# Moving GpSimd's work within a round of a product-key experts kernel, with wider pick sums and a later split of W_down

## The reference, cut to what matters

```python
q = (x @ Wq + bq).reshape(B, S, 8, 64)            # x = layernorm(x1)
s1 = einsum(q[..., :32], K1); s2 = einsum(q[..., 32:], K2)      # 64 scores each
v1, i1 = top_k(s1, 10); v2, i2 = top_k(s2, 10)
all_scores = v1[..., :, None] + v2[..., None, :]   # 100 sums a head
vals, best = top_k(all_scores, 10)                 # expert = i1 * 64 + i2
scores = softmax(vals)
h = gelu(x . W_down[expert]) * scores              # 8 heads x 10 experts
out = sum(h * W_up[expert])
result = x1 + layernorm(out)
```

## Time and profile before

| | us |
|---|---|
| median of 3 runs | 3631.82 |
| lowest, highest | 3631.26, 3637.74 |
| profiled execution | 3642.26 |
| its span | 3640.5 |

### The profile page before, as it was taken

How to read it: one execution, slowest core, us unless ns; L and a number is a source line. 1 busy time by engine, 2 the same in 40 slices (tenths; PEclk the granted TensorE clock), 3 DMA queues, 4 the chain that set the end, 5 groups by cost and what they waited for, 6 DMA issues and landing times. The chain is left out here.

```text
span 3640.5 us, 92336 instructions
## 1 busy us (share of the span) xinstructions
PE 3229.7 (89%) x31732; PEld 2786.5 (77%) x31732; DVE 3126.5 (86%) x15084; ACT 2134.9 (59%) x4411; POOL 2137.0 (59%) x1790
## 2 busy tenths in 40 slices
PE   5999999951499999999999899999999999999988
PEld 3666666631388888888888888888888888888888
DVE  5566666544899999999999999999999999999972
ACT  3444444411576766666666676666666666776662
POOL 1333333333366767666666677767766666676674
PEclk9999999975589999989988899989999888898988
DMA  2111111123033333333333333333333333333332
GB/s 62 47 53 53 53 53 53 41 76 156 30 117 116 118 118 114 103 104 116 103 103 119 104 126 115 120 114 109 103 117 103 103 103 120 120 119 111 117 117 97
DMA packets 132334, 356.93 MB, mean 98 GB/s; under 512 B 13865, under 2 KB 61609, under 8 KB 129452
## 3 DMA queue, kind: packets, MB, share of 16 engines
q1 hardware_dynamic: 131868, 351.03, 28.9%
HBM read 309.01 MB, written 25.17 MB: 92 GB/s over the span
## 5 line engine op out<-in xcount | busy, mean ns | idle before, releaser
L1182 PE MATMUL b_ps_a<-b_wup,b_hid 128*128 128x256 f32 x4096 | 955.9, 379 | 0.0
L1171 PE MATMUL b_ps_h<-b_xT_hi,b_wd_split 128*128 128x256 f32 x4096 | 931.8, 312 | 24.8 <-ACT b_hid L1322 21.5
L1010 POOL TENSOR_TENSOR b_hid<-b_hid,b_gates 128x512 f32<-128x512 f32 x512 | 717.4, 1401 | 297.1 <-ACT b_hid L1322 291.1
L1182 PEld LDWEIGHTS b_ps_a<-b_wup,b_hid 128*128 128x128 f32 x4096 | 743.4, 190 | 84.4 <-POOL b_hid L1010 0.3
L1171 PEld LDWEIGHTS b_ps_h<-b_xT_hi,b_wd_split 128*128 128x128 f32 x4096 | 709.2, 202 | 40.4 <-issue 31.1
L1301 ACT ACTIVATE b_ohq<-b_q_no,b_minus_qid 80x128 f16<-80x128 f16 x2048 | 648.1, 390 | 1.0
L1026 POOL TENSOR_TENSOR b_ohq<-b_qT 80x512 f16<-80x512 f16 x512 | 615.5, 1203 | 7.7 <-DVE b_qT L1422 7.7
L1171 PE MATMUL b_ps_h<-b_xT_lo,b_wd_split 128*128 128x256 f32 x2048 | 601.4, 294 | 0.0
L1098 PE MATMUL b_ps_s<-b_ohr,b_ohq 80*128 80x32 f16 x16384 | 445.4, 183 | 151.5 <-issue 151.3
L1098 PEld LDWEIGHTS b_ps_s<-b_ohr,b_ohq 80*128 80x128 f16 x16384 | 437.0, 101 | 158.3 <-issue 157.5
L1217 ACT ACTIVATE b_gates<-b_ps_s 128x512 f32<-128x512 f32 x512 | 305.6, 597 | 295.3 <-PE b_ps_s L1098 288.5
(11 more groups left out here) (192 smaller groups left out, 5518.0 us busy)
## 6 DMA issues: line engine op xcount, KB each, us to landing
b_wd_split<-wd_parts SPq DMA_DIRECT2D x512, 512.0 KB, 3.5
a_keysh<-a_key SPq DMA_DIRECT2D x16, 896.0 KB, 5.4
a_x<-in_x SPq DMA_DIRECT2D x16, 512.0 KB, 4.9
x_between<-a_y SPq DMA_DIRECT2D x16, 512.0 KB, 3.2
b_x<-x_between SPq DMA_DIRECT2D x32, 256.0 KB, 2.7
wd_parts<-b_wd_split SPq DMA_DIRECT2D x16, 512.0 KB, 3.1
b_x1t<-x_between SPq DMA_DIRECT2D x32, 256.0 KB, 4.1
out<-b_y SPq DMA_DIRECT2D x32, 256.0 KB, 2.3
```

Source lines behind the costliest of these rows:

```text
L1010: G.tensor_tensor(hid[:, p % 4, :, :], hid[:, p % 4, :, :], gates[:, 2 * p:2 * p + 2, :], ALU.mult).then_inc(mix_done, 1)
L1171: mm = T.matmul(hbank[p % 2][:, j * C:(j + 1) * C], a, c, start=i == 0, stop=i == len(parts) - 1)
L1182: mm = T.matmul(abank[:, t * D:(t + 1) * D], hid[:, p % 4, j, t * P:(t + 1) * P], wup[:, 2 * p + j, :], start=p == 0 and j == 0 and t == 0 ...
```

## The change

Six things are done together.

- GpSimd does 13 of the 16 mixes. VectorE does `mix(m, 13)` after the mask, `mix(m, 14)` after the product and `mix(m, 15)` after `onehots_r(m+1, 0)`. GpSimd's one-hot rows go in 13 portions of 5 tokens (the last of 4).
- On GpSimd `add_input(m-1)`, `low_x(m+2)` and `norm_in(m+3)` go behind mixes 0, 1 and 2; the first two thereby come a round later. SyncE's store and residual load move to p = 7 and 8.
- `sum_picks` takes three planes in one matmul: 9 matmuls of 480 columns. ScalarE copies three times as many columns, and `turn_picks` has 6 matmuls in place of 2, with 16-bit weights at a stride of six values.
- ScalarE's `soften(m+2)` goes ahead of `keep_gates(m+1)`; VectorE's goes from the lists of the next round to the end of the round; `turn_gates` goes from p = 4 to p = 1.
- The split of W_down: pieces 0 to 7 in round -2, pieces 8 to 15 in round -1, on ScalarE, GpSimd and SyncE. W_up is loaded after it.
- `low_gates` comes after pair 5 in place of 6, ahead of the one-hot portion.

```diff
-AT_GATES = 4
-AT_GLO, AT_CID = 6, 10
+AT_GATES = 1
+POOL_MIXES, DVE_MIXES = 13, 3
+WIDE = 3
+AT_GLO, AT_CID = 5, 10
...
         load(0)
-        keep_parts()
+        load_wdown()
         for m in range(-3, chunks + 1):
...
+            if m in (-3, -2):
+                keep_parts(m + 3)
+            if m == -2:
+                parts_kept()
...
-        for p in range(PAIRS_R):
-            low_down(p)
         for m in range(-3, chunks + 1):
             if has(m + 3):
                 root(0, m + 3)
-            if has(m + 3):
-                norm_in(m + 3)
-            for p in range(PAIRS_R):
+
+            if m in (-2, -1):
+                for p in range((m + 2) * PAIRS_R // 2, (m + 3) * PAIRS_R // 2):
+                    low_down(p)
+            for p in range(POOL_MIXES):
                 if has(m):
                     mix(m, p)
-                if has(m + 1):
-                    onehots(m + 1, p)
+                if p == 0 and has(m - 1):
+                    add_input(m - 1)
+                if p == 1 and has(m + 2):
+                    low_x(m + 2)
+                if p == 2 and has(m + 3):
+                    norm_in(m + 3)
                 if p == AT_GLO and has(m + 1):
                     low_gates(m + 1)
                 if p == AT_CID and has(m + 2):
                     pair_numbers(m + 2)
-            if has(m + 3):
-                low_x(m + 3)
+                if has(m + 1):
+                    onehots(m + 1, p)
             if has(m):
                 root(1, m)
-                add_input(m)
...
-            for c in range(NPAIR):
-                mm = T.matmul(rows, ident16[:, :], pk[:, :, c, :], start=c == 0, stop=c == NPAIR - 1)
+            for c in range(0, NPAIR, WIDE):
+                mm = T.matmul(rows, ident16[:, :], pk[:, :, c:c + WIDE, :], start=c == 0, stop=c == NPAIR - WIDE)
...
             for t in range(NT):
-                mm = T.matmul(mbank[0][0:SLOTS, t * P:(t + 1) * P], picked[:, t, :], ident16[:, :], start=True, stop=True)
+                for c in range(WIDE):
+                    mm = T.matmul(mbank[0][0:SLOTS, t * P:(t + 1) * P], picked[:, :, c, t], ident16[:, :],
+                                  start=c == 0, stop=c == WIDE - 1)
...
             if has(m + 3):
                 scores(m + 3)
+            if has(m + 2):
+                soften(m + 2)
             if has(m + 1):
                 for b in range(BLOCKS):
                     keep_gates(m + 1, b)
-            if has(m + 2):
-                soften(m + 2)
...
+        def mix(m, p):
+            dve.wait_ge(gelu_done, m * PAIRS_R + p + 1)
+            dve.wait_ge(gates_done, GROUPS * (m + 1))
+            V.tensor_tensor(hid[:, p % 4, :, :], hid[:, p % 4, :, :], gates[:, 2 * p:2 * p + 2, :], ALU.mult).then_inc(mix_dve_done, 1)
...
-            if has(m + 1):
-                soften(m + 1)
...
-                pick(m + 2)
+                mask(m + 2)
+            if has(m):
+                mix(m, POOL_MIXES)
+            if has(m + 2):
+                product(m + 2)
+            if has(m):
+                mix(m, POOL_MIXES + 1)
             if has(m + 1):
                 onehots_r(m + 1, 0)
+            if has(m):
+                mix(m, POOL_MIXES + 2)
+            if has(m + 1):
                 onehots_r(m + 1, 1)
                 onehots_q(m + 1, 2)
...
             if has(m + 1):
                 onehots_r(m + 1, 3)
+            if has(m + 2):
+                soften(m + 2)
```

More of the change, by code:

```diff
@@ L831, in experts_phase @@
     posf = sb("b_posf", [P, SLOTS, NT], F16)
-    picked = sb("b_picked", [P, NT, SLOTS], F16)
+    picked = sb("b_picked", [P, SLOTS, WIDE, NT], F16)
     gate = sb("b_gate", [P, NT, SLOTS], F32)
@@ L877, in experts_phase @@
     ohq_pool_done, cid_done, glo_done = (sem(f"b_{n}") for n in ("ohq_pool", "cid", "glo"))
+    mix_dve_done = sem("b_mix_dve")
     eps_done = [sem(f"b_eps{i}") for i in range(2)]
@@ L935, in load, with load_wdown, keep_parts, parts_kept @@
             sp.dma_start(x1[:, :, :], x1_view[m]).then_inc(x1_in, 16)
-        def keep_parts():
+        def load_wdown():
             sp.dma_start(wdown, w["wdown"].rearrange("(k p) r q -> p k r q", p=P)).then_inc(wdown_in, 16)
-            sp.dma_start(wup[:, :, :], w["wup"]).then_inc(wup_in, 16)
-            for p in range(PAIRS_R):
+        def keep_parts(half):
+            for p in range(half * PAIRS_R // 2, (half + 1) * PAIRS_R // 2):
                 sp.wait_ge(wd_lo_done, p + 1)
                 sp.dma_start(wd_dram[p], whole_slot(p)).then_inc(wd_out[p % WD_SLOTS], 16)
+        def parts_kept():
+            sp.dma_start(wup[:, :, :], w["wup"]).then_inc(wup_in, 16)
             for i in range(WD_SLOTS):
@@ L968, in sp_program @@
                     load_down(m, p)
-                if p == 1 and has(m - 1):
+                if p == 7 and has(m - 1):
                     store(m - 1)
-                if p == 2 and has(m):
+                if p == 8 and has(m):
                     load_residual(m)
@@ L1019, in onehots @@
         def onehots(m, p):
-            n = BLK // PAIRS_R
-            tok = slice(p * n, (p + 1) * n)
-            shape = [SLOTS, n, 16, 8]
+            tok = slice(p * 5, min(p * 5 + 5, BLK))
+            shape = [SLOTS, tok.stop - tok.start, 16, 8]
             pool.wait_ge(oh16_done, m + 1)
@@ L1086, in gate_matrix @@
             if b == 0:
-                pe.wait_ge(ohq_pool_done, PAIRS_R * (m + 1))
+                pe.wait_ge(ohq_pool_done, POOL_MIXES * (m + 1))
             elif b == 1:
@@ L1115, in sum_picks @@
             pk = work.rearrange("p (s c t) -> p s c t", s=SLOTS, c=NPAIR)
-            rows = mbank[1][:, 0:NT * SLOTS].rearrange("p (s t) -> p s t", t=NT)
+            rows = mbank[1][:, 0:NT * WIDE * SLOTS].rearrange("p (s c t) -> p s c t", c=WIDE, t=NT)
             pe.wait_ge(picks_done, m + 1)
@@ L1175, in up @@
             n = m * PAIRS_R + p
-            pe.wait_ge(mix_done, n + 1)
+            if p < POOL_MIXES:
+                pe.wait_ge(mix_done, POOL_MIXES * m + p + 1)
+            else:
+                pe.wait_ge(mix_dve_done, DVE_MIXES * m + p - POOL_MIXES + 1)
             pe.wait_ge(wup_in, 16)
@@ L1211, in keep_gates @@
             if m:
-                act.wait_ge(mix_done, PAIRS_R * m)
+                act.wait_ge(mix_done, POOL_MIXES * m)
+                act.wait_ge(mix_dve_done, DVE_MIXES * m)
             else:
@@ L1235, in turn_picks @@
                 act.wait_ge(picked_pe, m)
-            S.copy(picked[:, :, :].rearrange("p t s -> p s t"),
-                   mbank[1][:, 0:NT * SLOTS].rearrange("p (s t) -> p s t", t=NT)).then_inc(picked_done, 1)
+            S.copy(picked[:, :, :, :].rearrange("p s c t -> p (s c t)"),
+                   mbank[1][:, 0:NT * WIDE * SLOTS]).then_inc(picked_done, 1)
         def turn_gates(m):
@@ L1255, in queries @@
                 if m >= 2:
-                    act.wait_ge(ohq_pool_done, PAIRS_R * (m - 1))
+                    act.wait_ge(ohq_pool_done, POOL_MIXES * (m - 1))
                 bank = sbank[fills["q", m, half] % 3]
@@ L1322, in gelu @@
             S.activation(hid[:, p % 4, :, :], hbank[p % 2][:, :].rearrange("p (j c) -> p j c", j=2), ACT.Gelu).then_inc(gelu_done, 1)
-        for p in range(PAIRS_R):
-            high_down(p)
         for m in range(-3, chunks + 1):
+            if m in (-2, -1):
+                for p in range((m + 2) * PAIRS_R // 2, (m + 3) * PAIRS_R // 2):
+                    high_down(p)
             for p in range(PAIRS_R):
@@ L1416, in decode @@
             if m:
-                dve.wait_ge(ohq_pool_done, PAIRS_R * m)
+                dve.wait_ge(ohq_pool_done, POOL_MIXES * m)
             V.tensor_tensor(oh8[:, :, :], field8[:, :].unsqueeze(2).to_broadcast([SLOTS, BLK, 8]),
@@ L1528, in pairs_top, with mask @@
             op.then_inc(pairs_done[t], 1)
-        def pick(m):
+        def mask(m):
             dve.wait_ge(pairs_done[NT - 1], 5 * (m + 1))
@@ L1544, in pick, with product @@
                             ALU.is_equal).then_inc(mask_done, 1)
+        def product(m):
             w4 = work.rearrange("p (h k c) -> p h k c", h=HEADS, k=TOPK)
```

1 line of the change is left out of this document (removed).

## The result

The kernel after takes 3730.73 us (median of 4 runs, 3727.52 to 3738.72), the kernel before 3634.55 in the same runs: ratio 1.0264, interval 1.0249 to 1.0279. It is slower by 96 us; forecast was 3574, 60 us faster.

The account below looks back on a forecast made before the run. VectorE's program was taken to set the round, TensorE close behind. Lead-in -38.5, 29 rounds -16, round 29 -4 and round 30 +1 gave -58 us: 3574 us, range 3505 to 3645.

Parts of the forecast that it names:

- VectorE's own sum: VectorE's work in a round: 83.4 less 5.9 of stalls plus 1.9 for three mixes, 79.4 us.
- It just fits; an overlap costs up to 1.3 a time: GpSimd beside the lists: 40 us of work ends at 41.7, the mask starts at 42.4.
- the slower one: Rival, 10%: TensorE goes cold at mix 15 and stays cold through up(15), queries and scores; 3699 us.
- The queue's end: GpSimd's 40 us of work beside the lists ends at t = 41.7, before the mask at 42.4.
- The ring: Mix 15 late, TensorE idle 2.5 us, gates late behind soften, VectorE waits before onehots_r(2); round 80.1 us plus the sums.
- clock link: After TensorE's 2.5 us idle the clock falls, costing about 1.4 us every other round: 0.7 a round.
- the rival of the queue that runs past the lists: Rival, 10%: GpSimd's steps hit mask and product, 1 to 2 us a round; 3600 to 3632 us.
- The wide sums: The nine pick-sum matmuls on TensorE take 2.2 us in place of 4.29, a run priced at one and a half pairs.
- Mixes on VectorE: Three mixes added to VectorE's round, 0.63 us each from start to start, 1.9 a round.
- Stalls removed: VectorE's delays in onehots_r(0), onehots_r(3) and the product go: 4.0, 0.95 and 0.95, together 5.9 us.
- Lead-in: Before the rounds, root(0, 0) no longer stands behind W_down's split: 38.5 us earlier, nothing lost later.

Follow-up runs that it names:

- numbers after 7: The changed kernel with GpSimd's pair_numbers after its mix 7 in place of mix 10: 3644.39 us, ratio 1.0025 to the kernel before.

## Why the prediction was wrong

- **The step that failed** is VectorE's own sum together with "It just fits; an overlap costs up to 1.3 a time". I checked GpSimd's queue only against the mask and what follows, and carried the lists over at their old length, though by my own sum the change put 40 us of GpSimd work without a gap beside them: for what that work does to the lists the sum has no term. Two kinds of instruction in the lists are held up by GpSimd: the conversions and the pair sums. One overlap cost 6.1 us (6.36 against 0.25), five GpSimd instructions, not one. Taking it away gives back 86 of the 157 us between forecast and result. A row of the trace could have warned me: the conversion at 1949.10 took 1.06 and ended in GpSimd's hole. That row alone fits both prices, one instruction and the time to the next pause; the runs show that it is the second. No rival had it; the slower one had its place at mix 15.
- **The queue's end**, forecast t = 41.7, is 42.2 (1978.94): right, and beside the mask no use, since the mask had itself gone to 48.0.
- **The ring** is there: mix 15 late, TensorE idle before `up(15)`, the stop at the first gate copy (1.32), VectorE's wait of 3.35 (forecast some 3; 93.0 us in 27 rounds). Its clock link isn't in the sampled round of the kernel after: there the idle of 3.57 and the fall stand before `up(13)`, and TensorE still has to wait for mix 15, so the fall costs the ring nothing. Without my 0.7 for it the part behind the mask would have been forecast at 40.0, and 39.8 were measured. With the blocked conversion gone, in "numbers after 7", the ring is right in every link, the clock too. What moving one instruction gives there (-113 us, 3.9 a round; forecast 83.1 against 79.4 for VectorE's own sum, 3.7) measures it. That kernel takes 3644, still 70 over the forecast: the round is 85.2, against 83.1, with the mask 1.4 later (shift and casts under GpSimd's end, the rival of the queue that runs past the lists), and 0.7 more behind it. The clock explains that 0.7 by size: it falls in eight of nine rounds at 1.6 to 1.7, 1.5 a round, where I took 1.4 in every other one. No run takes the fall away by itself.
- **The wide sums:** 2.15 us from start to start (2000.25 to 2002.40), forecast 2.2. The one and a half pairs for a run of six values were a guess between two bounds, so that it came out is luck. Nine instructions in place of 27 are no other explanation of the size: the gate matrix's matmuls follow each other every 26 ns, so 18 fewer are worth 0.5 us at most, and 2.1 were gained. The Trainium skill (SBUF — State Buffer, the note on cachelines in Door 1) says that two hits in a line are enough for full bandwidth, which would have left 4.3; this trace doesn't agree. The same note has a penalty for each access that crosses to a new line, and that is the way in which these rows go.
- **Mixes on VectorE** 0.60 from start to start, forecast 0.63. **Stalls removed:** 5.9, as forecast (`onehots_r(0)` 3.64 and `onehots_r(3)` 3.65 from start to start, the product 2.32).
- **Lead-in:** `root(0, 0)` 814.20, 37.8 earlier (forecast 38.5), first mask 869.9, 38.3 earlier, second mask 933.9, 34.1 earlier. The 4 us go in round -2, where I took nothing: VectorE waits 9.22 us for ScalarE's `soften` behind the lists, before 8.14 for TensorE with `soften` hidden in them. With the split alone none of it is lost (masks at 867.6 and 927.0, 40.6 and 41.0 earlier), so these us are the price of the other edits, not of the split.

On the lock itself: the Trainium skill (SBUF — State Buffer, Who interferes with whom) says that a VectorE instruction in a two-port mode, or with two inputs in SBUF while GpSimd reads there, contends with GpSimd for a shared port pair: whoever issues first gets it for the whole instruction, and the other blocks. The trace agrees that one blocks. The block doesn't end with one GpSimd instruction, though, which would be 1.3 us here: single VectorE instructions took 6.3, 11.3 and 7.0 us. That it is this port pair, no run shows.

## What to carry to other kernels

A hole in one engine's queue can be what lets another engine in: before closing it, list every instruction of the other engine that will now run beside a gapless queue, and price each at the time to the next pause, not at one instruction. A wait of GpSimd placed so that it stands 1.1 to 2.3 us there while VectorE's sensitive instruction goes through serves as that pause; where it stood 4.76, the gain was waited away. And when a forecast names a ring with an idle link, try the order that removes the link first: here one moved instruction was worth 113 us.

## What the hardware showed

- A VectorE conversion of 0.245 us beside back-to-back GpSimd instructions took 6.36 (x28) and, with two pairs more (4.9 us) ahead of GpSimd's next wait, 11.33 us (x25). Which rule of arbitration does this was not measured; that a GpSimd queue with starts 1.23 apart and durations of 1.28 leaves no gap is what the rows show.
- Among five GpSimd additions of 0.24 to 0.49 us a blocked VectorE sum was released at 2034.44, without a pause; that short instructions let VectorE in more readily is a guess from this, not tested by a run of its own.
- TensorE's granted clock was 0.51 after an idle of 3.57 us, and 0.54 after one of 2.25 us, where eight matmuls took 3.41 in place of 1.83; the same idle of 2.25 left it alone in one round of nine.
